# AdaLN block with windowed attention and a routed low-rank FFN on one core: modulation in the weights, normalised x turned by DMA, fp16 low-rank products, two pairs of score banks

## What is computed

```python
h = _layernorm(x, axis=-1) * (1 + ca) + sa
x = x + ga * _L0_attn_ref(h, ...)
h = _layernorm(x, axis=-1) * (1 + cb) + sb
x = x + gb * _L0_ffn_ref(h, ...)
```

## Time and profile before

| what | us |
|---|---|
| median of 3 executions | 522.66 |
| lowest, highest | 520.54, 524.2 |
| the profiled execution, its own time | 522.22 |
| its span, first to last instruction | 520.4 |
| PE busy in it | 459.0 |

### The profile page before, as it was taken

How to read it: one execution, slowest core, us unless ns; L and a number is a source line. 1 busy time by engine, 2 the same in 40 slices (tenths; PEclk the granted TensorE clock), 3 DMA queues, 4 the chain that set the end, 5 groups by cost and what they waited for, 6 DMA issues and landing times.

```text
span 520.4 us, 10871 instructions
## 1 busy us (share of the span) xinstructions
PE 459.0 (88%) x4112; PEld 294.1 (57%) x4112; DVE 334.1 (64%) x597; ACT 302.9 (58%) x966; POOL 287.1 (55%) x320
## 2 busy tenths in 40 slices
PE   2949998999799999999999999999979999973756
PEld 0227664667577657856765757756645664532422
DVE  3486788899877776777775575575548677425110
ACT  1532755797687878775686636576548665512200
POOL 3264373271667363457656666856736796815811
PEclk9968999999899999999999999999999999997979
DMA  8992132732342424423262434354253464530141
GB/s 329 354 375 86 42 82 42 230 95 42 82 97 68 82 62 88 77 62 82 56 128 42 103 60 96 91 82 103 62 122 72 92 131 78 118 82 26 35 101 42
DMA packets 110292, 53.32 MB, mean 102 GB/s; under 512 B 100768, under 2 KB 100896, under 8 KB 109856
## 3 DMA queue, kind: packets, MB, share of 16 engines
q1 hardware_dynamic: 110096, 52.60, 40.9%
q10 hardware_dynamic: 144, 0.02, 0.1%
HBM read 23.25 MB, written 4.19 MB: 53 GB/s over the span
## 4 chain that ended last, share of the span: by engine, by line
PE 57%; DVE 12%; issue 8%; ACT 8%; POOL 7%; DMA 7%; SPq 1%; POOLq 0%; ACTq 0%; DVEq 0%
PE F L842 15%; PE C L924 14%; PE C L842 10%; PE S L964 3%; DMA xb<-in_x_dram 3%; PE WB L981 3%; ACT prob L589 3%; PE WB L842 3%; PE S L958 2%; PE F L892 2%; DVE p L768 2%; DMA gT<-g 2%; PE S L892 2%; PE T L1005 2%; DMA wma<-in_wmod_dram 2%
## 5 line engine op out<-in xcount | busy, mean ns | idle before, releaser
L924 PE MATMUL C<-hT,cw 128*128 128x256 f16 x864 | 106.5, 277 | 3.5 <-POOL hT L426 3.2
L924 PEld LDWEIGHTS C<-hT,cw 128*128 128x128 f16 x864 | 83.9, 99 | 22.7 <-POOL hT L426 4.7
L842 PE MATMUL F<-btw,gT 128*128 128x512 f16 x384 | 87.8, 386 | 9.8 <-DMA gT<-g 9.8
L589 ACT ACTIVATE prob<-S,nms 128x128 f32<-128x128 f32 x256 | 89.9, 378 | 7.6 <-DVE p L768 6.8
L473 POOL TENSOR_TENSOR prob<-prob,rinv 128x1024 f32<-128x1024 f32 x32 | 61.5, 1923 | 46.7 <-DVE rinv L773 46.6
L560 ACT ACTIVATE qk<-C,bqk 128x256 f16<-128x256 f32 x128 | 52.7, 480 | 31.6 <-PE C L842 31.3
L842 PEld LDWEIGHTS F<-btw,gT 128*128 128x128 f16 x384 | 37.6, 100 | 55.5 <-DMA gT<-g 11.6
L748 DVE SCALAR_TENSOR_TENSOR qk<-C,bqk,qk 128x256 f16<-128x256 f32 x128 | 54.7, 475 | 14.8 <-ACT qk L560 14.4
L842 PE MATMUL C<-cv,pw 128*128 128x256 f16 x384 | 52.8, 281 | 8.2 <-DVE xb L789 3.6
L589 ACT ACTIVATION_READ_ACCUMULATOR prob<-S,nms 128x1 f32 x256 | 55.6, 217 | 0.0
L768 DVE SCALAR_TENSOR_TENSOR p<-prob,p 128x1024 f16<-128x1024 f32 x32 | 46.5, 1452 | 6.5 <-ACT p L598 6.2
(11 more groups left out here) (140 smaller groups left out, 775.1 us busy)
## 6 DMA issues: line engine op xcount, KB each, us to landing
xa<-in_x_dram SPq DMA_DIRECT2D x8, 512.0 KB, 4.1
xb<-in_x_dram SPq DMA_DIRECT2D x8, 512.0 KB, 4.7
out_dram<-xb SPq DMA_DIRECT2D x16, 256.0 KB, 2.1
wmb<-in_wmod_dram SPq DMA_DIRECT2D x1, 3072.0 KB, 14.3
cw_raw<-in_cw_dram SPq DMA_DIRECT2D x3, 768.0 KB, 11.9
wma<-in_wmod_dram SPq DMA_DIRECT2D x1, 2048.0 KB, 8.7
bt_raw<-in_btw_dram SPq DMA_DIRECT2D x2, 1024.0 KB, 8.7
pw_raw<-in_pw_dram SPq DMA_DIRECT2D x3, 512.0 KB, 15.8
```

The costliest lines, as they stand in the source:

```text
L589: ins = nc.scalar.activation(prob[:, h], S[h // 4][:, (h % 4) * P:(h % 4 + 1) * P], ACT.Exp, bias=nms[:, i % 2, h:h + 1], scale=S_SCALE, a ...
L842: ins = nc.tensor.matmul(dst, stat(a), mov(b), start=first and i == 0, stop=last and i == 2)
L924: ins = nc.tensor.matmul(bank_c[:, 0:CH], cw[:, i, a, tap, c, :], hT[:, j % 2, b, c, tap:tap + CH], start=step == 0, stop=step == STEPS - 1)
```

## The change

- **Modulation.** LayerNorm's output is no longer scaled and shifted. (1 + ca) goes into the convolution's weights, (1 + cb) into `bsw` and `arw`, as the per-partition scale of their split, in four pieces for the four parts of 512 channels; as the two batches differ, the weights are loaded and split again for batch 1 (`ra`, `sp:0:11` to `sp:0:16`) in the middle of the program. The shifts become biases: `vb` (sa through the convolution, per tap), `fbias` (sb through `bsw`), `lb` (sb through `arw`). Tokens at a batch's edge lack a tap, so the first and last chunk of a batch evacuate one column of the convolution by itself (`spans`).
- **Columns.** `cols` has its values from 32 fp32 matmuls, a 128x128 piece of wmod as the weight and the 2 columns of silu(c) moving; the rows 0, 1, 3, 4 and the transposes go. The load of wma is four DMAs, behind both first x chunks.
- **Turning x.** Normalised x is split where it lies, token-major: ACT the high half (`hs`, L600), POOL the low (L519), and two DMA transposes of 128x1024 each bring it to `hT`, the same for `h2` (`hs2`). No fp32 copy, no PE transposes, no T banks.
- **Low-rank products** are fp16 in three passes from `h2` with `arw`, through a C bank; DVE reads them and adds the bias.
- **Score banks.** The two T banks become a second pair of S banks, used in turn.
- **Order.** `SCHEDULE` is written anew. Loads of the first chunks are issued in another order: the later weights behind the transposes of chunk 1.

The core of the diff:

```diff
 
     SCHEDULE = """
-        sil:0:0 na:0:0 nb:0:0 na:1:0 row:0:0 row:0:1 nb:1:0 cols:0:0 ln:0:0 sp:0:0 sp:0:2 mod:0:0 row:0:2 ln:1:0
...
+        na:0:0 nb:0:0 hs:0:0 sil:0:0 na:1:0 nb:1:0 halo:0:0 hs:1:0 halo:1:0 cols:0:0 vb:0:0 sp:0:0 c:0:9 sp:0:1
+        c:0:18 sp:0:2 sp:0:3 c:0:9 na:2:0 vb:0:1 vb:0:2 c:0:27 sp:0:4 c:0:9 qk:0:1 nb:2:0 row:0:2 qk:0:4 c:0:15
...
-        S = [psum(f"S{i}") for i in range(2)]
-        T = [psum(f"T{i}") for i in range(2)]
+        S = [[psum(f"S{i}{h}") for h in range(2)] for i in range(2)]
...
+        def conv_split(n, src, b, loaded):
+            return [(cw[:, n, HI, c], cw[:, n, LO, c], src[:, c], by_c(1, b)[c]) for c in range(DC)], loaded
...
+        SPLITS = [conv_split(n, cw_raw[:, n], 0, (ld[f"cw{n}"], 16)) for n in range(3)]
...
+        def spans(j):
+
+            at, to = (1 if j % CPB == 0 else 0), (CH - 1 if j % CPB == CPB - 1 else CH)
+            return [(0, at, to)] + [(1, 0, 1)] * at + [(2, CH - 1, CH)] * (CH - to)
...
+            for i in range(2):
+                sp.dma_start(xa[:, i], xin[i]).then_inc(ld_xa[i], 16)
+            for c in range(DC):
+                sp.dma_start(wma[:, c, 0:2, :], wmod_v[:, c, 0:2, :]).then_inc(ld[f"wma{c}"], 16)
+            sp.dma_start(cw_raw[:, 0], cw_in[:, 0]).then_inc(ld["cw0"], 16)
...
+                if s == "hs":
+
+                    sp.wait_ge(h_lo, j + 1)
+                    if j >= 2:
+                        k, idx = bank(C_USE["c", j - 2, 2])
+                        sp.wait_ge(c_full[k], idx + 1)
+                        sp.wait_ge(h_ready, H_DONE[j - 1])
+                    for b in range(2):
+                        sp.dma_start_transpose(
+                            hT[:, j % 2, :, :, OWN + b * P:OWN + (b + 1) * P].rearrange("p m c q -> p (m c) q"),
+                            h16[:, b].rearrange("p m d -> p (m d)")).then_inc(h_moved, 16)
+                    if j == 1:
+                        for n in range(1, 3):
+                            sp.dma_start(cw_raw[:, n], cw_in[:, n]).then_inc(ld[f"cw{n}"], 16)
+                        for n in range(3):
+                            sp.dma_start(pw_raw[:, n], pw_in[:, n]).then_inc(ld[f"pw{n}"], 16)
...
+                        for i in range(2):
+                            sp.dma_start(xa[:, i], xin[i + 2]).then_inc(ld_xa[i], 16)
+                            sp.dma_start(xb[:, i], xin[i]).then_inc(ld_xb[i], 16)
...
+                elif s == "hs2":
+                    sp.wait_ge(h2_lo, j + 1)
+                    if j > 0:
+                        sp.wait_ge(fb_read, 2 * j)
+                        k, idx = bank(C_USE["lr", j - 1, 0])
+                        sp.wait_ge(c_full[k], idx + 1)
+                    for b in range(2):
+                        sp.dma_start_transpose(h2[:, :, :, b * P:(b + 1) * P].rearrange("p m c q -> p (m c) q"),
+                                               h216[:, b].rearrange("p m d -> p (m d)")).then_inc(h2_moved, 16)
...
+                elif s == "ra":
+
+                    if n == 0:
+                        sp.wait_ge(split_lo, split_by(10))
+                        sp.wait_ge(m_done, mod_by(("fbias", 0), ("fbias", 1), ("lb", 0), ("lb", 1)))
+                    else:
+                        sp.wait_ge(split_lo, split_by(N_FIRST + n - 1))
+                    dst, src = [(raw_cw, cw_in[:, 0]), (raw_cw, cw_in[:, 1]), (raw_cw, cw_in[:, 2]),
+                                (raw_bs, bsw_in[:, 0:2]), (raw_bs, bsw_in[:, 2:4]), (raw_ar, ar_in)][n]
+                    sp.dma_start(dst, src).then_inc(ld["raw"], 16)
...
-                elif s == "mod":
...
+                elif s == "hs":
+                    pool.wait_ge(h_hi, j + 1)
+                    nc.gpsimd.tensor_tensor(h16[:, :, LO], xa[:, j % 2], h16[:, :, HI], ALU.subtract).then_inc(h_lo, 1)
+                elif s == "halo":
+                    pool.wait_ge(h_moved, 32 * (j + 1))
...
+                elif s == "hs2":
...
-                    nc.gpsimd.tensor_tensor(h2[:, LO], hf2[:], h2[:, HI], ALU.subtract).then_inc(h2_ready, 1)
...
+                    parts, loaded = SPLITS[n]
+                    act.wait_ge(*loaded)
+                    split_waits(act, n)
+                    for dst, _, src, scale in parts:
+                        ins = nc.scalar.activation(dst, src, ACT.Copy, scale=scale)
+                    ins.then_inc(split_hi, 1)
...
+                elif s == "hs":
+                    act.wait_ge(xn_ready, 2 * j + 2)
...
+                        act.wait_ge(h_moved, 32 * j)
+                    nc.scalar.activation(h16[:, :, HI], xa[:, j % 2], ACT.Copy).then_inc(h_hi, 1)
...
+                    for kind, at, to in spans(j):
+                        ins = nc.scalar.activation(cv[:, n[0], HI, at:to], C[k][:, at:to], ACT.Identity,
+                                                   bias=cbias[:, n[0], kind, batch(j):batch(j) + 1])
+                    ins.then_inc(cv_hi, 1)
...
+                elif s == "lr":
+                    k, idx = bank(C_USE[stage])
+                    dve.wait_ge(c_full[k], idx + 1)
...
+                    nc.vector.scalar_tensor_tensor(out=lr[:], in0=C[k][:, 0:2 * ARW].rearrange("p (b a) -> p b a", b=2),
+                                                   scalar=1.0 / FFN_SCALE,
+                                                   in1=lrb[:, batch(j)].unsqueeze(1).broadcast_to([P, 2, ARW]),
+                                                   op0=ALU.mult, op1=ALU.add).then_inc(c_done[k], 1)
...
-                            at = (m * DC + k) * NB
-                            ins = nc.tensor.transpose(m_bank(stage)[:, at:at + NB], row_ab[:, m, k * P:(k + 1) * P],
-                                                      ident[0:NB, 0:NB])
+                        for c in range(DC):
+                            at = (m * DC + c) * NB
+                            for k in range(DC):
+                                if m == c == 0:
+                                    pe.wait_ge(ld[f"wma{k}" if n == 0 else "wmb"], 16)
+                                ins = nc.tensor.matmul(m_bank(stage)[:, at:at + NB],
+                                                       (wma if n == 0 else wmb)[:, k, m, c * P:(c + 1) * P],
+                                                       silT[:, 0, k * NB:(k + 1) * NB], start=k == 0, stop=k == DC - 1)
...
+                elif s == "vb":
...
+                    for tap in range(TAPS):
+                        for c in range(DC):
+                            ins = nc.tensor.matmul(m_bank(stage)[:, tap * NB:(tap + 1) * NB], cw_raw[:, n, c, tap, :],
+                                                   modT[:, 0, c, :], start=c == 0, stop=c == DC - 1)
+                    ins.then_inc(m_full, 1)
+                elif s == "fbias" or s == "lb":
...
+                    held, wide = (bs_raw, D) if s == "fbias" else (ar_raw, ARW)
+                    for c in range(DC):
+                        ins = nc.tensor.matmul(m_bank(stage)[:, 0:wide], modT[:, 2, c, n:n + 1].broadcast_to([P, P]),
+                                               held[:, c, :], start=c == 0, stop=c == DC - 1)
...
+                        if j == CPB:
+                            pe.wait_ge(split_lo, split_by(N_FIRST + i))
+                    c, tap, (a, b) = step // (3 * TAPS), step // 3 % TAPS, PASSES[step % 3]
+                    ins = nc.tensor.matmul(bank_c[:, 0:CH], cw[:, i, a, c, tap, :],
+                                           hT[:, j % 2, b, c, OWN - 1 + tap:OWN - 1 + tap + CH],
                                            start=step == 0, stop=step == STEPS - 1)
...
-                        pe.wait_ge(s_done, i)
+                        pe.wait_ge(s_done, i - len(S) + 1)
...
                 elif s == "lr":
-                    for g in range(2):
-                        t_wait(T_USE["x2", j, 0] + g)
-                    if j == 0:
-                        pe.wait_ge(ld["ar"], 16)
-                    k = t_bank(T_USE[stage])
+                    pe.wait_ge(h2_moved, 32 * (j + 1))
+                    if j % CPB == 0:
+                        pe.wait_ge(split_lo, split_by(10 if j == 0 else N_FIRST + 5))
+                    k = c_bank(C_USE[stage])
                     for b in range(2):
                         for c in range(DC):
-                            ins = nc.tensor.matmul(T[k][:, b * ARW:(b + 1) * ARW], hf2[:, c, b * P:(b + 1) * P], arT[:, c, :],
-                                                   start=c == 0, stop=c == DC - 1)
-                    ins.then_inc(t_full[k], 1)
+                            ins = passes(C[k][:, b * ARW:(b + 1) * ARW], lambda m: h2[:, m, c, b * P:(b + 1) * P],
+                                         lambda m: arw[:, m, c, :], c == 0, c == DC - 1)
```

442 lines of the change are left out of this document (210 added, 232 removed).

## The result

The changed kernel takes 517.56 us in the median of 17 runs (514.39 to 521.04), the one before 520.86 (17 runs, 519.34 to 524.2): a ratio of 0.993, interval 0.9911 to 0.995. It is faster by 0.7%, 3.3 us between the medians, where I had forecast 511, 11.7 less than 522.66. The interval leaves out 1, but by the 1% that the prediction takes for a change this is "same", which it gave 0.15. The profiled execution of the changed kernel, the lower side of its runs, took 516.02 us (span 513.9), against 522.22 (span 520.4). Medians and ranges leave out executions over 1.5% above the fastest of their kernel: 4 of 12 of the kernel that spreads the column stage, 9 of 11 of the one that covers that spread, 2 of 8 of the one with a filled wait, and none elsewhere.

The account below looks back on a forecast made before the run. PE work was taken as the bound from 60 to 450 us, with start and end priced separately. Span 520.4 - 10.5 (PE work) + 3.1 (start) + 0 (middle) - 4 (end) = 509.0, forecast as 511 us, range 498 to 522.

Parts of the forecast that it names:

- same: Whole kernel: a time within about 1% of no change, neither below 517.4 us nor over 527.9; given 0.15.
- my range: Whole kernel: forecast time 511 us, with a range of 498 to 522.
- The sign that I had set: Start: the prediction counts as wrong if the convolution starts after 31 us; 26.9 was forecast.
- I take 0.11: PE work: each two-column fp32 record of `cols` and `vb` costs 0.11 us, 22 us for those two items.
- my sum: PE work added by the new groups: 40.5 us, against 51.0 removed, net -10.5.
- the low clock in `cols`: Start: 2.4 us for the low clock, counted within PE's idle time of 22.2 us up to 64 us.
- The start's end at 26: Start, weight path: `vb` and the scaled split of cw0 end at 26 us.
- the path of x: Start: normalised x split, transposed and halo-copied, ready at 26.9 us, so the convolution starts 10.5 us sooner.
- Idle time: PE idle: 22.2 us to 64 us against 19.1 before to 60 (+3.1), middle kept at 17.1 (+0).
- The end: After 450 us: x ready about 3.5 us sooner, low-rank product at 481, G about 486.5; sum -4 us.
- the low-rank groups: PE work: 8 x 24 fp16 matmuls with 80 columns at 0.05 us, 9.6 us (5.9 to 29).
- with no slack: Start, DVE: x_2's statistics stand ahead of an evacuation; queries come to 45 us as PE ends row 0:2, nothing lost.

## Why the prediction was wrong, and where it was right

**Direction right, size not**: 0.7% instead of 2.2%. That 517.56 lies inside my range is in part luck: on the spans PE's work was 11.4 us more than forecast, and idle time 6.5 less. The sign that I had set (wrong if the conv starts after 31) came: 36.11. The parts:

- **The step that failed: "I take 0.11"** for a two-column fp32 record. The price holds at the high clock (0.12 in the 48 records at 41.93) and is double at the low one. 64 + 24 records at the start at 0.217 instead of 0.11 are 9.4 us, the second column stage 3.1 more (10.1 for 7.0), `vb` 1 and 2 another 0.5: 13.0, against the 12.9 measured between all groups and my sum. I had written 2.4 us for "the low clock in `cols`" into the idle time, for the first of them only. I took the row with 80 columns as the price of a weight load and did not ask at which clock it ran (the trace has 1.00 there, from 480 to 484 us), nor at which the new ones would. The prediction's own rows held the warning: wide fp32 matmuls 0.62 us each from rest and 0.45 in the run.
- **A low clock costs wide matmuls too, but that is not in this error.** The two conv thirds at the start took 5.98 and 5.39 us instead of 4.12; the kernel before paid about as much there, 10.81 for the same 72 matmuls, and all 864 took 105.9 us now and 106.5 before.
- **The start's end at 26** failed by the same term, and by the queue: my working lets the split end at 26 beside `vb`, but DVE's split stands behind `vb`'s evacuation in its queue (33.77), and silT came 1.7 us late. Conv at 36.11 for 26.9. With 48 of the records left out it starts at 27.32, so the path of x was worked out right (26.8 measured, 26.9 forecast).
- **Idle time came out better than my terms**: up to 60 us 17.1 for 22.2 (PE was busy with slow records instead), the middle 14.9 for 17.1. Sum on the spans: PE's work +0.9 (forecast -10.5), idle time -2.0, -2.2, -3.3 (forecast +3.1, 0, -4): -6.6, and the spans differ by 6.5.
- **The end was right from x_7's normalised x on**: POOL's subtraction done at 474.5 (475.5), the pair of turns landed 4.6 us after its first issue (4.3), low-rank product done at 480.95 (481), G at 486.23 (486.5); idle 3.3 us less for a forecast 4. Ahead of it the times were not: the last transpose of p went at 449.35 (452.8) and the reload at 451.32 (455), 62.6 us before the end, where I had set 58 to 62. And I had laid all of these times on the old kernel's, which holds only because the changed one had gained about 1 us by then (450.32 before), not the rest of my sum.
- **Right too**: the low-rank groups 9.0 us (9.6), `fbias` 7.3 (7.1), and `na:2` "with no slack": put six words later in the list it costs 8.1 us.
- The rest of the distance between the forecast and the median is the mark. I set the sum against one execution of 522.22 us; over 17 runs the kernel before has 520.86, and the changed one's profiled 516.02 lies 1.5 below its median.

**The spread goes with the clock.** Over the 17 runs of the changed kernel, the same instructions took 521.04 us with a mean granted clock of 0.961 and 515.63 with 0.976, and over all 17 the longer ones are mostly those with the lower clock. The ends are 6.7 us apart, 4.9 for the kernel before. That more falls make a kernel less steady would fit, but was not tested.
